# Second cross attention, last 20 steps: every second step's probabilities are split by VectorE

## The reference, cut to what matters

```python
def _L1_xattn_ref(query, key, value, mask, Wq, bq, Wk, bk, Wv, bv, Wo, bo):
    q = proj(query, Wq, bq)
    k = proj(key, Wk, bk)
    v = proj(value, Wv, bv)
    score = jnp.einsum('bhqd,bhkd->bhqk', q, k) * scale
    score = jnp.where(m == 0, jnp.asarray(-1000000000.0, score.dtype), score)
    p = jax.nn.softmax(score, axis=-1)
    x = jnp.einsum('bhqk,bhkd->bhqd', p, v)
    return x @ Wo.T + bo
```

## Time and profile before

| | us |
|---|---|
| median of 3 runs | 2471.84 |
| lowest and highest | 2466.27, 2475.08 |
| the profiled execution | 2460.13 |
| its span | 2458.0 |

### The profile page before, as it was taken

One profiled execution on the slowest core, in us unless ns is written; L12 is line 12 of the kernel. 1 busy time (PEld: TensorE's weight loads), 2 busy tenths in 40 slices (PEclk: granted clock), 3 DMA queues, 4 the chain that ended last, 5 costly groups with the idle time before them and its releaser, 6 DMA issues. The chain is left out here.

```text
span 2458.0 us, 57983 instructions
## 1 busy us (share of the span) xinstructions
PE 2254.2 (92%) x22147; PEld 1469.9 (60%) x22147; DVE 1835.7 (75%) x3392; ACT 1591.6 (65%) x2938; POOL 1135.8 (46%) x903
## 2 busy tenths in 40 slices
PE   6999999999999999998898699995799999998696
PEld 3456656666566656665455577772567677776452
DVE  5777878887788877777565899995777777767437
ACT  5556666666666666665364599983467777788523
POOL 3446676666765665555200000003467677656420
PEclk9999999999999999998899799997999999999897
DMA  6323332224222321123430799984533434224202
GB/s 211 105 54 94 113 87 73 74 68 132 83 70 82 104 81 39 37 62 119 161 129 24 261 369 365 361 315 146 173 122 121 137 119 129 90 89 136 79 1 88
DMA packets 247252, 313.59 MB, mean 128 GB/s; under 512 B 63152, under 2 KB 171568, under 8 KB 246080
## 3 DMA queue, kind: packets, MB, share of 16 engines
q1 hardware_dynamic: 242496, 298.87, 37.7%
q10 hardware_dynamic: 3840, 8.91, 1.0%
q0 software_dynamic: 640, 2.10, 0.3%
HBM read 226.23 MB, written 47.91 MB: 112 GB/s over the span
## 5 line engine op out<-in xcount | busy, mean ns | idle before, releaser
L587 POOL TENSOR_TENSOR a_late<-a_late 128x512 bf16<-128x512 f32 x272 | 318.2, 1170 | 356.8 <-ACT a_late L645 356.1
L986 PE MATMUL ps<-w,a_xhi 128*128 128x512 bf16 x1088 | 413.8, 380 | 5.5 <-POOL a_xlo L560 5.5
L987 PE MATMUL ps<-w,a_xhi 128*128 128x512 bf16 x1088 | 413.9, 380 | 0.0
L988 PE MATMUL ps<-w,a_xlo 128*128 128x512 bf16 x1088 | 413.8, 380 | 0.0
L2425 POOL TENSOR_TENSOR a_plo<-a_p,a_phi 128x512 bf16<-128x512 f32 x256 | 307.0, 1200 | 170.3 <-ACT a_phi L2462 161.2
L611 ACT ACTIVATE a_kraw<-ps 128x256 f32<-128x256 f32 x272 | 104.4, 384 | 369.3 <-PE ps L988 367.6
L2557 DVE CUSTOM_DVE_ANT_0 a_junk<-ps,a_biasrow 128x512 bf16<-128x512 f32 x256 | 176.1, 688 | 106.8 <-PE ps L2697 103.9
L723 DVE TENSOR_TENSOR a_v<-ps,a_v 128x256 bf16<-128x256 f32 x272 | 114.5, 421 | 152.3 <-ACT a_v L613 150.9
L2457 ACT ACTIVATE a_p<-ps,a_mcol 128x512 f32<-128x512 f32 x256 | 175.0, 683 | 79.0 <-PE ps L2715 71.5
L544 POOL TENSOR_TENSOR a_rn<-a_rn,a_power 128x16 f32<-128x16 f32 (+1 forms) x80 | 204.1, 2551 | 6.7
L737 DVE SCALAR_TENSOR_TENSOR a_kraw<-a_kraw,a_rn 128x1024 f32<-128x1024 f32 (+1 forms) x80 | 152.3, 1903 | 73.5 <-POOL a_rn L544 73.5
(11 more groups left out here) (496 smaller groups left out, 6952.3 us busy)
## 6 DMA issues: line engine op xcount, KB each, us to landing
e_wst<-in_L_ffn_W SPq DMA_DIRECT2D x46, 2048.0 KB, 10.7
a_ks<-a_khi SPq DMA_DIRECT2D x256, 64.0 KB, 2.0
a_ks<-a_klo SPq DMA_DIRECT2D x256, 64.0 KB, 2.0
a_ct<-in_ctxT SPq DMA_DIRECT2D x16, 1024.0 KB, 5.6
a_ks<-k1h_d SPq DMA_DIRECT2D x128, 128.0 KB, 2.5
xa<-in_ctx SPq DMA_DIRECT2D x8, 1024.0 KB, 6.0
a_xn<-in_ctx SPq DMA_DIRECT2D x8, 1024.0 KB, 6.1
k1h_d<-a_khi SPq DMA_DIRECT2D x64, 128.0 KB, 1.9
```

The costliest lines, as they stand in the source:

```text
L587: pool.tensor_tensor(p_lo[:, m % 3, :], p32[:, m % 2, :], p_hi[:, m % 3, :], ALU.subtract)\
L986: pe.matmul(out, x_hi[:, c, tile], w_hi[:, c, g, :], start=(c == 0), stop=False)
L987: pe.matmul(out, x_hi[:, c, tile], w_lo[:, c, g, :], start=False, stop=False)
L988: last = pe.matmul(out, x_lo[:, c, tile], w_hi[:, c, g, :], start=False, stop=(c == C - 1))
```

## The change

Steps 237, 239, ..., 255 (ten in all) get both parts of their probabilities on VectorE. ScalarE leaves out their rounding, GpSimd their subtraction; VectorE gets `parts(m)`, a cast and a subtraction, at iteration m + 26, ahead of that iteration's `copy_turned` and `add_result` and behind its `add_bias`. Who waited for such a step's low part (the exponential of step m + 2 and `values(m)`) waits for VectorE in its place. All other steps are as they were.

```diff
+    DRAIN = N - C1LAG + 6
...
+    def on_vector(m):
+        return m >= DRAIN and m % 2 == 1
...
                 m = n - C1LAG
-                if 0 <= m < N:
-                    pool.wait_ge(phi_done, m + 1)
+                if 0 <= m < N and not on_vector(m):
+                    pool.wait_ge(phi_done, parts_count(m))
...
                 if m >= 2:
-                    act.wait_ge(plo_done, m - 1)
+                    act.wait_ge(*parts_of(m - 2, plo_done))
                 act.activation(p32[:, m % 2, :], ps[:, m % 2, :], ACT.Exp, bias=mcol[:, u // 4, s:s + 1])\
                    .then_inc(exp_done, 1)
+                if on_vector(m):
+                    return
...
+            def parts(m):
+                dve.wait_ge(exp_done, m + 1)
+                dve.wait_ge(pv_mm, m - 2)
+                step(dve.tensor_copy(p_hi[:, m % 3, :], p32[:, m % 2, :]))
+                dve.tensor_tensor(p_lo[:, m % 3, :], p32[:, m % 2, :], p_hi[:, m % 3, :], ALU.subtract)\
+                   .then_inc(parts_done, 1)
...
                 if BACK - B <= n < BACK:
                     add_bias(n - BACK + B)
+                if on_vector(n - C1LAG) and n - C1LAG < N:
+                    parts(n - C1LAG)
                 b, s = divmod(n - BACK, 3)
                 if s == 0 and 0 <= b < B:
                     copy_turned(b, 0, C if b < B - 1 else C - 1)
...
-                pe.wait_ge(plo_done, m + 1)
+                pe.wait_ge(*parts_of(m, plo_done))
```

More of the change, by code:

```diff
@@ L2251, in cross1_attend @@
     s_mm, exp_done, phi_done, plo_done, pv_mm = sem("a1_s"), sem("a1_exp"), sem("a1_phid"), sem("a1_plod"), sem("a1_pv")
-    o_evac, ao_ready = sem("a1_o"), sem("a1_aor")
+    o_evac, ao_ready, parts_done = sem("a1_o"), sem("a1_aor"), sem("a1_parts")
     ao_out = [sem("a1_ao_out0"), sem("a1_ao_out1")]
@@ L2281, in cross1_attend, with parts_count, parts_of @@
     row_of = {NT * u + 24: u for u in range(4 * B)}
+    def on_vector(m):
+        return m >= DRAIN and m % 2 == 1
+    def parts_count(m):
+        return (m - DRAIN + 1) // 2 if on_vector(m) else m + 1 if m < DRAIN else DRAIN + (m - DRAIN) // 2 + 1
+    def parts_of(m, elsewhere):
+        return (parts_done if on_vector(m) else elsewhere), parts_count(m)
     def max_index(u, j, h):
```

## The result

The changed kernel takes 2472.47 us (median of 22 runs, 2466.28 to 2483.03), the kernel before 2467.24 (22 runs, 2460.20 to 2476.52). The ratio is 1.0023, 95% interval 1.0012 to 1.0033: slower by 5.7 us, between 3 and 8, a quarter of a per cent. (The kernel before had 2471.84 from its first three runs; 22 runs put it 4.6 us lower.)

What follows compares the result with a forecast made beforehand. Bounds: VectorE's full list, then TensorE's pace, then the last steps' chain. Terms 2.1 + 0.8 (clock) + 2.2 - 0.5 = +4.6 us on 2471.8 gave 2476.4 us; eight in ten: 2466 to 2484.

Steps and rivals of the forecast that it cites:

- No difference that shows: Whole kernel: 2476.4 us, 0.19% more, within the 0.3% a measurement can tell, with a lean to slower; chance 0.60.
- Part one, the list of VectorE: 2268.5 to 2278.4 us: VectorE never rests, so added pairs delay the first copy and first product by +2.1 us (+0.9 to +4.7).
- the three pairs: Casts and subtractions of steps 237, 239 and 241 on VectorE ahead of the first copy: 3.4 us clean together.
- The contacts themselves: Part one: GpSimd's subtraction of step 238 makes the first bias end 0.55 us later; step 240's meets pair 239, taking 1.1.
- The tiles' 0.95 us earlier end: Start of part one: without GpSimd's subtraction of step 237, the fourth diagonal tile ends at about 2269.7, not 2270.65.
- The clock: TensorE's first product: all four passes at 1.2 GHz, 3.6 us to the next scores, +0.8 us (-0.9 to +0.9).
- Part two: 2278.4 to 2299.1 us, TensorE sets the pace: second and fourth copies behind pairs +1.1 each, third nothing; +2.2 (0 to +4.4).
- GpSimd's and ScalarE's relief: Part two: work taken from ScalarE and GpSimd shortens nothing, since ScalarE waits there for the scores.
- Part three: 2299.1 to 2305.4 us, last three steps: moved work lies on the chain of exponential, rounding, subtraction, values; -0.5 us (-0.8 to 0).
- The relief: Rival 1, mainly part one: lock freed from GpSimd exceeds the pairs' need; sum +0.3 or -0.8 us, 2471 to 2472; chance 0.17.
- The lock as a price of each half: Rival 2: GpSimd's subtraction starts ahead of each pair half; pair mean about 2 us, +10.8 us, 2482.6; chance 0.17.
- the change does little: Rival 3: pairs wait for late exponentials with VectorE free, only the end differs; 2471.3 us; chance 0.06.

Runs made afterwards that it cites:

- four: Changed kernel with the four output-bias additions moved behind the first copy: first copy at 12.29 us, stretch (exponential 235 to last addition to xa) 47.26, time ratio 1.0015.
- the first trace: First profiled execution of the changed kernel, against the kernel before: exponential of step 235 to last addition to xa 48.46 us, before 44.56.
- the second trace: The same changed kernel profiled again, nothing altered: first copy at 14.39 us, exponential of step 235 to last addition to xa 49.46 us.
- five: Changed kernel plus twelve idle matmuls, six ahead of step 239's values, six ahead of the first product: exponential 235 to last addition to xa 47.00 us, from 48.46.
- One: Changed kernel with the transposed-batch copy ahead of the pair, not behind it: exponential 235 to last addition to xa 47.11 us; ratio to kernel before 1.0024.
- six: Changed kernel without GpSimd's subtractions of even steps from 236 on, a one-column memset instead: first copy at 11.88 us, exponential 235 to last addition to xa 44.53.
- Seven: Kernel before with only steps 253 and 255 getting their parts from VectorE: exponential 235 to last addition to xa 44.37 us, time ratio 1.0000.
- eight: Kernel before with only steps 253, 254 and 255 getting their parts from VectorE: exponential 235 to last addition to xa 43.63 us, time ratio 0.9997.

## Why the prediction held

The forecast was +4.6 us, the ratio says +5.7 (3 to 8), the two traces +3.9 and +4.9. The 2476.4 us were too high by 3.9 because its starting point, the median of three runs, was 4.6 above that of 22. "No difference that shows" holds by the 0.3% that the prediction named as its limit (0.23% measured), but not against 22 runs of each kernel, whose interval of 0.1% to each side leaves 1 outside: the lean to slower was real.

- **Part one, the list of VectorE.** Right in its cause: biases moved away, the copy came 1.5 to 2.1 us earlier (four). Its size was 1.54 in the first trace and 2.16 in the second, forecast 2.1. The prediction's list has the first copy 14.41 us behind exponential 235, and the first trace 13.77. What it sized wrong is the pairs and the result: the three pairs took 1.06, 1.90 and 1.07 us to the start of the next instruction where it had 1.15, 2.10 and 1.20, and the result 1.49 where it had 1.75 with some contact with GpSimd. The contacts themselves (first bias, step 239's subtraction) fell as it said. That the second trace's 14.39 is nearly its number is luck: there other instructions were blocked, for 2.6 us where it had 2.15, and the rest was shorter. The tiles' 0.95 us earlier end proved 0.83 and 0.94.
- **The clock.** Forecast +0.8, measured +0.63 and +0.81, and shown by five, and by four, where the start was the same and the clock was not.
- **Part two.** Forecast +1.1, 0, +1.1; measured +1.02, 0, +1.12, and the same within 0.01 in the second trace. One shows that the place in the list makes it, six that the lock has no share. That GpSimd's and ScalarE's relief is worth nothing there also held: they only idle longer.
- **Part three.** Forecast -0.5, measured -0.40; the last cast is blocked to 0.90 us as foreseen. Seven against eight show that the remaining GpSimd step keeps the larger part (0.27 with two pairs, 1.05 with three). The Trainium skill (Perfetto Trace Analysis, Optimizing Scalar/DVE Operations) doubts that moves between VectorE and GpSimd help. In this part the trace doesn't agree: the moved work gains 0.40 us in the changed kernel, and 1.05 where no GpSimd instruction is left beside it.
- **Rivals.** The relief does not win: it would have needed the first copy under +1. The lock as a price of each half falls with the pair's mean of 1.3 us (0.52 + 0.77), not 2. That the change does little falls with the table.

What stays open: which of the two ways the pairs fall together with GpSimd is the more frequent (three traces had the first copy at 14.38 or 14.39, two at 13.77 or 13.78), and which of TensorE's waits costs the clock. The ratio's excess over the first trace, 1.8 us, lies inside its interval, and the second trace covers half of it.

## What to carry to other kernels

An instruction moved to an idle engine costs what stands behind it in that engine's list, even while it waits: a pair of 1.14 us put ahead of a copy of 0.69 delayed TensorE by 1.1 us, though VectorE was idle for 5.85 us before it. Before moving work off an engine, look which wait ends last in each part of the stretch; here the time went through the engines that were relieved only in the last three steps, and relieving only those, completely and not by halves, was the part that paid. And a wait of TensorE can have a second price behind it, in the clock of the next matmuls.

## What was not expected of the hardware

- Idle matmuls in TensorE's waits brought the first product from 3.37 us at a granted clock of 0.5 to 1.80 at 1.0. They cost nothing where they fit into the wait, and 1.2 us where six of them ran at half clock ahead of values that were due.
- The same lists fall together in more than one way: VectorE's first copy at 13.77 or 14.39 us, the second product piece 3.82 or 4.32 us behind the first, in the same kernel. A difference of 0.12 us in the start of one bias goes with those 0.6 us. A term worked out from one trace to a tenth of a microsecond is no more certain than 0.6.
- Everything ahead of the stretch moved by up to 15 us between executions (exponential 235 at 2263.1 to 2278.7), four times the effect studied. The difference of two spans said 19.0 us, the stretch 3.9.
